# A transformer layer on eight cores: replication matmuls in bf16 and the second layernorm's sums of squares moved into the output-projection loop

## The reference

```
x = x + attn(layernorm(x))          # softmax(q k^T / 8) v, then @ wo.T + bo
h = silu(layernorm(x) @ w1.T * s1) * (layernorm(x) @ w2.T * s2)
h = gelu(h @ h1.T * sh1); h = gelu(h @ h2.T * sh2)
x = x + h @ w3.T * s3
layernorm(x) = (x - mean) / sqrt(var + 1e-5)     # no learned scale
```

## Time and profile before

| | |
|---|---|
| median of 10 runs | 3755.22 us |
| the profiled execution | 3755.95 us |
| its span, slowest core (core 2) | 3754.4 us |
| spans of the 8 cores | 3738.1 to 3754.4 us |
| TensorE busy | 3371.8 us, 90% |
| VectorE busy | 481.5 us, 13% |
| ScalarE busy | 805.2 us, 21% |

### The profile page before, as it was taken

How to read it: one execution, slowest core, us unless ns; L and a number is a source line. 1 busy time by engine, 2 the same in 40 slices (tenths; PEclk the granted TensorE clock), 3 DMA queues, 4 the chain that set the end, 5 groups by cost and what they waited for, 6 DMA issues and landing times.

```text
span 3754.4 us, 35126 instructions; the slowest of 8 cores (3738.1 to 3754.4 us)
## 1 busy us (share of the span) xinstructions
PE 3371.8 (90%) x14708; PEld 1390.9 (37%) x14708; DVE 481.5 (13%) x469; ACT 805.2 (21%) x741; POOL 151.7 (4%) x290
## 2 busy tenths in 40 slices
PE   2378888888878499999999999999999999999999
PEld 0122222222222144444444444444444444444444
DVE  0523222222132503000000000000310000000000
ACT  1114777777800230000000000003000000000000
POOL 0000000000000011000000000001100000000000
PEclk9689999999859699999999999999999999999999
DMA  7000000001005054544443444455554444444444
GB/s 157 0 0 1 1 1 1 1 1 23 1 23 165 17 78 75 89 77 79 79 74 72 79 79 76 82 137 76 76 93 75 73 77 79 77 72 76 79 79 129
DMA packets 49612, 237.44 MB, mean 63 GB/s; under 512 B 7777, under 2 KB 7842, under 8 KB 28338
## 3 DMA queue, kind: packets, MB, share of 16 engines
q0 software_dynamic: 40176, 193.04, 30.0%
q1 hardware_dynamic: 9282, 42.15, 3.3%
HBM read 411.19 MB, written 16.78 MB: 114 GB/s over the span
## 4 chain that ended last, share of the span: by engine, by line
PE 65%; DVE 1%; DMA 1%; ACT 0%; issue 0%; DVEq 0%; ACTq 0%; POOLq 0%
PE ps_f L1041 65%; DMA wb<-h 1%; DVE act_bf L194 1%; PE ps_m L978 0%; PE ps_r L982 0%; ACT hbufA L1065 0%; DVE ostg L1092 0%; ACT hbufB L1065 0%; DVEq L193 0%; ACTq L1057 0%; DVEq L1091 0%; DVEq L1089 0%; DVEq L1079 0%; DVEq L1078 0%; POOLq L1009 0%
## 5 line engine op out<-in xcount | busy, mean ns | idle before, releaser
L1041 PE MATMUL ps_f<-hbufB,wb 128*128 128x512 bf16 x5120 | 1109.7, 380 | 11.5 <-DMA wb<-h 8.5
L1041 PE MATMUL ps_f<-hbufA,wb 128*128 128x512 bf16 x4096 | 884.4, 379 | 2.9 <-ACT hbufA L1065 2.9
L1041 PEld LDWEIGHTS ps_f<-hbufB,wb 128*128 128x128 bf16 x5120 | 501.7, 98 | 619.5 <-issue 18.6
L731 ACT ACTIVATE pbuf<-ps_sc,cneg 128x1024 bf16<-128x1024 f32 x512 | 531.3, 1132 | 268.4 <-PE ps_sc L437 266.5
L1041 PEld LDWEIGHTS ps_f<-hbufA,wb 128*128 128x128 bf16 x4096 | 400.6, 98 | 486.7 <-issue 3.9
L1041 PE MATMUL ps_f<-act_bf,wb 128*128 128x512 bf16 x2048 | 445.6, 381 | 4.6 <-ACT hbufA L1065 2.8
L458 PE MATMUL ps_aE<-pbuf,vt_sb 128*65 128x512 bf16 x512 | 220.1, 430 | 86.6 <-DVE q_sb L715 85.4
L1041 PEld LDWEIGHTS ps_f<-act_bf,wb 128*128 128x128 bf16 x2048 | 200.9, 98 | 250.3 <-issue 11.3
L1092 DVE SCALAR_TENSOR_TENSOR ostg<-ps_f,s_sb,x2rb 128x1024 f32<-128x1024 f32 x16 | 20.5, 1284 | 1988.2 <-PE ps_f L1041 1988.2
L1065 ACT ACTIVATE hbufB<-ps_f,sh_sb 128x1024 bf16<-128x1024 f32 x64 | 71.3, 1114 | 816.0 <-PE ps_f L1041 816.0
L1065 ACT ACTIVATE hbufA<-ps_f,sh_sb 128x1024 bf16<-128x1024 f32 x64 | 71.3, 1114 | 784.8 <-PE ps_f L1041 784.8
(11 more groups left out here) (94 smaller groups left out, 998.1 us busy)
## 6 DMA issues: line engine op xcount, KB each, us to landing
wb<-h POOLq DMA_DIRECT2D x128, 1024.0 KB, 8.0
wb<-w POOLq DMA_DIRECT2D x128, 256.0 KB, 3.8
wb<-w POOLq DMA_DIRECT2D x16, 1024.0 KB, 8.9
xrb<-xst SPq DMA_DIRECT2D x8, 1024.0 KB, 5.3
x2hbm<-x2buf SPq DMA_DIRECT2D x8, 1024.0 KB, 16.0
x2rb<-x2hbm SPq DMA_DIRECT2D x16, 512.0 KB, 9.1
out_fm<-ostg SPq DMA_DIRECT2D x16, 512.0 KB, 8.5
wqld<-wq POOLq DMA_DIRECT2D x1, 2048.0 KB, 16.3
```

The costliest lines, as they stand in the source:

```text
L731: sc.activation(pbuf[:, (c % 4) * 1024:(c % 4) * 1024 + 1024], ps_sc[:, (c % 2) * 1024:(c % 2) * 1024 + 1024], AF.Exp, bias=cneg[:, j:j + ...
L1041: ins = t.matmul(ps_f[:, (i % 2) * 1024 + nn * 512:(i % 2) * 1024 + (nn + 1) * 512], wb[i % 3][:, k * 128:(k + 1) * 128], rhs[:, k * rstri ...
```

## The change

Two parts.

The replication stage: `selpair` and `rtile` become bf16. The reciprocal is now taken in place in `denom_sb`, and a `tensor_copy` casts it into `rtile`. The DMA that loads `selpair` converts from f32, and is now issued by GpSimd, in the attention block behind the same wait (`s_vt`), and no longer by SyncE.

The wo loop: one PSUM tensor `ps_stats` [33, S] takes both sums, that of x in row 0 and that of the squares in row 32. ScalarE squares all 8 chunks inside the loop, and TensorE sums the squares of chunk m-3 at the end of iteration m (for m of 3 or more), and the last three behind the last x sum. The block of stage 5 keeps only the row chain. GpSimd's wait for the weight loads keeps its number, 23, while `s_pe` now counts 32 steps in this block and no longer 24.

```diff
-    selpair_sb = arena("selpair", [16, NPAIR * 128], F32)
+    selpair_sb = arena("selpair", [16, NPAIR * 128], BF16)
-    rtile = arena("rtile", [16, S], F32)
+    rtile = arena("rtile", [16, S], BF16)
...
+                    if j == 0:
+                        @blk.gpsimd
+                        def _(g):
+                            g.wait_ge(s_vt, TC)
+                            g.dma_start(selpair_sb, selpair_c).then_inc(s_small, 16)
                     @blk.sync
                     def _(sy, j=j, I0=I0):
-                        if j == 0:
-                            sy.wait_ge(s_vt, TC)
-                            sy.dma_start(selpair_sb, selpair_c).then_inc(s_const, 16)
...
-                    vop(v, "reciprocal", rtile, denom_sb)
+                    vop(v, "reciprocal", denom_sb, denom_sb)
+                    vop(v, "tensor_copy", rtile, denom_sb)
...
-                    t.wait_ge(s_const, 48)
+                    t.wait_ge(s_small, 16 * 11)
...
-        with nc.psum_tensor("ps_sxb", [1, S], F32) as ps_sxb:
+        with nc.psum_tensor("ps_stats", [33, S], F32) as ps_stats:
...
+                        def emit_stats_sq(k):
+                            t.wait_ge(s_sc, sq0 + k + 1)
+                            ins = None
+                            for nn in range(4):
+                                ins = t.matmul(ps_stats[32:33, nn * 512:(nn + 1) * 512],
+                                               onescol_bf,
+                                               sqbf2[:, (k % 2) * S + nn * 512: (k % 2) * S + (nn + 1) * 512],
+                                               start=(k == 0), stop=(k == KD - 1))
+                            ins.then_inc(s_pe, 1)
+                            n["pe"] += 1
+                            sqstat_pe[k] = n["pe"]
...
                             if m >= 1:
                                 emit_stats_sx(m - 1)
+                            if m >= 3:
+                                emit_stats_sq(m - 3)
                         emit_stats_sx(KD - 1)
-
-                    n["pe"] += 2 * KD + KD
+                        for k in range(KD - 3, KD):
+                            emit_stats_sq(k)
...
-                                v.wait_ge(s_pe, pe0 + g2 + 1 + max(m - 1, 0))
+                                v.wait_ge(s_pe, pe0 + g2 + 1 + max(m - 1, 0) + max(m - 3, 0))
...
-                        for k in range(2):
+                        for k in range(KD):
                             sc.wait_ge(s_v, v0 + 2 * k + 2)
+                            if k >= 2:
+                                sc.wait_ge(s_pe, sqstat_pe[k - 2])
                             scop(sc, "activation", sqbf2[:, (k % 2) * S:(k % 2) * S + S],
                                  x2buf[:, k * S:(k + 1) * S], AF.Square)
...
-            with nc.psum_tensor("ps_sqb", [1, S], F32) as ps_sqb:
-                with nc.Block() as blk:
-                    sq1 = n["sc"] - 2
-                    pe1 = n["pe"]
...
+            with nc.Block() as blk:
                     @blk.vector
                     def _(v):
                         v.wait_ge(s_pe, n["pe"])
```

More of the change, by code:

```diff
@@ L796, in build_nc @@
                     sq0 = n["sc"]
+                    sqstat_pe = {}
                     @blk.gpsimd
@@ L820, in emit_stats_sx @@
                             for nn in range(4):
-                                ins = t.matmul(ps_sxb[:, nn * 512:(nn + 1) * 512],
+                                ins = t.matmul(ps_stats[0:1, nn * 512:(nn + 1) * 512],
                                                onescol_sb,
@@ L851, in _ @@
                                 g2 = 2 * m + hf
-                                v.wait_ge(s_pe, pe0 + g2 + 1 + max(m - 1, 0))
+                                nsx = max(m - 1, 0) if hf == 0 else max(m, 0) if m == 0 else max(m - 1, 0)
+                                v.wait_ge(s_pe, pe0 + g2 + 1 + max(m - 1, 0) + max(m - 3, 0))
                                 v.wait_ge(sxr[m % 2], 16 * (m // 2 + 1))
@@ L906, in _ @@
                         rowu = xsq2[0:1, S:2 * S]
-                        vop(v, "tensor_scalar_mul", rowm, ps_sxb[:], 1.0 / D)
+                        vop(v, "tensor_scalar_mul", rowm, ps_stats[0:1, :], 1.0 / D)
                         vop(v, "tensor_mul", rowu, rowm, rowm)
-                        vop(v, "scalar_tensor_tensor", rowr, ps_sqb[:], 1.0 / D,
+                        vop(v, "scalar_tensor_tensor", rowr, ps_stats[32:33, :], 1.0 / D,
                             rowu, ALU.mult, ALU.subtract)
```

## The result

The changed kernel takes 3701.08 us (median of 9 runs, the lowest 3696.93 us) against 3754.85 us (median of 32 runs of before). The ratio is 0.985, with a 95% interval of 0.984 to 0.9861: about 56 us faster.

A forecast was written before the change was run, and what follows sets the result against it. It took TensorE to bound the replication stage and wo loop, then GpSimd's drain the block's end. Gains of 34.9 and 19.5 us, 54.4 in all, from 3755.95 gave 3701.6, so a median of 3701 us, range 3695 to 3709.

The forecast's parts named there:

- The cast is 1.21 us, 2.28 at most: Replication stage: the added f32-to-bf16 cast of 16x2048 was taken as 1.21 us, with 2.28 as the other end.
- A bf16 group of four takes 1.71 us at half clock, and VectorE becomes the bound: Replication stage: four matmuls take 1.71 us in place of 6.83, VectorE's multiplies then narrowly bound it; gain 34.9 us.
- The rival that kept 0.854 us for each matmul: Replication stage: bf16 on 16 rows keeps the f32 instruction's time, groups take 3.41 us, TensorE still bounds; 3709 us, 7%.
- Each sum of squares stands on TensorE's path in full, 0.86 us, 6.9 in all: Wo loop and its tail: TensorE is the bound, so 8 groups at 0.86 us add 6.9 us.
- The rival of parallel sums: Wo block: squares' sums in row 32 run beside the x sums; 5.2 us more gained, 3696 us, 6%.
- Square 7 waits for its buffer: Wo block's tail: the seventh square starts only after squares 5 is summed, at 1209.67; TensorE is done at 1212.75.
- The weight loads, issued at 1194.6, land in 13 us and are hidden: Wo block's end: the third load lands at 1207.6, 5 us before TensorE is done, so it costs nothing.
- the 12% rival: Wo block's end: a load among the stores takes 23.3 us, GpSimd's drain sets the barrier; 5.0 us lost, 3706 us, 12%.
- The chain starts at 95.8 us on this scale: After the wo block's barrier: VectorE's row chain starts at 1213.3 against 1232.75, a gain of 19.5 us.
- A block's end waits for GpSimd's transfers and not for SyncE's: Wo block's end: GpSimd's drain lasts until its third weight load lands; SyncE's took 0.13 us with a store under way.
- The clock comes back in the loop: Wo loop: TensorE's clock rises from 0.50 as before; the rival that it stays there gave 3790 us, 2%.
- Some tenths for each switch between sums: Wo loop: some tenths of a us for each switch between sums, allowed within the forecast's own range of 3698 to 3704.

The follow-up runs named there:

- the late loads: The changed kernel with the first three weight loads issued at count 31 in place of 23, behind the last but one sum; 3702.38 us in its only run.

## Why the prediction came out right, and where its steps did not

The time was right, 3701 forecast and 3701.08 measured, and so was the mechanism of the first part. But two of the second part's steps were wrong, in opposite directions: 5.4 us too much for TensorE, 2.8 us too little for the barrier. That the sum still came within 3 us is luck, and the agreement to 0.1 us is more of it, since the mean of the runs is 3698.7 us.

- *The cast is 1.21 us, 2.28 at most.* Measured 1.22. The nearest row, a one-source operation between SBUF tensors, was the right one.
- *A bf16 group of four takes 1.71 us at half clock, and VectorE becomes the bound.* Measured 1.86 with the last one's end, no idle time between the multiplies, 22.64 us for the stage where 22.8 were forecast. Gain 35.0 for 34.9. The rival that kept 0.854 us for each matmul is out. The moved load of `selpair` cost nothing: TensorE started 0.25 us behind the cast, as forecast.
- *Each sum of squares stands on TensorE's path in full, 0.86 us, 6.9 in all.* Wrong. I drew it from the first layernorm, where both sums go to row 0 and so follow one another. In row 32 they are free behind an x sum; only the last, which stands alone, costs time. TensorE's last sum ended 89.9 us after the loop's start and not 95.3, 5.4 earlier: 5.2 by the parallel sums, 0.9 by a clock that rose sooner, less 0.6 by a slower last group. The rival of parallel sums had this mechanism and its price, 5.2 us, at 6%. I took it for unlikely for two reasons, and both misled me. One was that only one of the four instructions would have an x matmul next to it; all four started before the last two of the x sum. The other was that one engine's instructions follow one another in every row. That holds for the rows I showed, but not for the trace of before. In the attention the two score matmuls of a head pair, whose operands lie on partitions 0 to 63 and 64 to 127, take 0.39 us together, no more than one matmul of the line behind them, where two that follow one another take 0.59 (the pairs of line 837 above):

```profile
1000.42 0.39 PE L437 MATMUL ps_sc<-q_sb,k_sb 64*128 64x512 bf16 x2
1000.74 0.41 PE L458 MATMUL ps_aE<-pbuf,vt_sb 128*65 128x512 bf16 x1
1000.99 0.38 PE L458 MATMUL ps_aO<-pbuf,vt_sb 128*65 128x512 bf16 x1
```

What no row of before could show is a pair of one-column sums in two strips, since all of them wrote to row 0.
- *Square 7 waits for its buffer.* Right: ScalarE idles 1.52 us for it, and TensorE 2.25 us for ScalarE. The last group then took 1.65 us and not 1.02; the granted clock from 1172.20 to 1173.90 was 0.58. With the late loads, behind the same 2.25 us of idle time, it was 1.00, and the group took 1.02.
- *The weight loads, issued at 1194.6, land in 13 us and are hidden.* Wrong: 18.9 us. I had carried the 13.0 over from a place behind the last store to one among the stores, although the prediction named 23.3 as the other end. The drain ended 2.8 us after TensorE's, and held the chain until 93.2 us. This is the mechanism of the 12% rival, at 2.8 us in place of its 5.0; so the two rivals came true together and nearly cancelled.
- *The chain starts at 95.8 us on this scale* (1213.3 - 1117.4). Measured 93.2, which is 5.4 earlier for TensorE and 2.8 later for GpSimd's drain. The second part gained 22.1 us where 19.5 were forecast.
- *A block's end waits for GpSimd's transfers and not for SyncE's.* Right: in every kernel here SyncE's drain at the end of the wo block took 0.13 us or less with stores under way, and without GpSimd's the chain started 0.6 us behind TensorE's last sum.
- *The clock comes back in the loop.* Right; it is 0.97 over the loop again, as before.
- *Some tenths for each switch between sums.* None were seen: the iterations with sums of squares take 10.53 us, like those of before.

## What to carry to other kernels

Read the drains at each block's end. A GpSimd drain of tens of microseconds can be a wait for transfers that nobody behind the barrier needs yet. If whoever needs them waits for their own semaphore, as here, the drain can go: in the first block that was worth 39 us, against 56 for the whole change. Put a one-column sum into a PSUM row of another strip than the one-column sum in front of it (row 32 against row 0 is what was tried here), and not between full-width matmuls. When a transfer is moved, take its duration from the traffic at its new place. And before a rival is called unlikely because no row shows its mechanism, look through the other stages of the trace for it.

## What the hardware showed that I had not expected

- Two one-column matmul groups in different strips of the array (rows 0 and 32 of the output) ran side by side and added nothing: 10.53 us an iteration against 11.40 in the same strip.
- TensorE's records are then not in program order: a sum of squares started at 1122.51, ahead of an x sum's instruction at 1122.93 that stands before it in the program.
- Of three loads of 256 KB each, issued back to back, the third landed after 9.5 to 13.0 us behind the stores of 1 MB, 11.5 to 12.0 ahead of them and 18.4 to 20.3 among them. Whether they lose that time in the DMA engines or in memory was not tried.
- GpSimd's drain at a block's end lasted until its last transfer had landed (40.2 us in the first block of the changed kernel); SyncE's took 0.1 us there, with the 8 MB of x under way.
